# L1f: normalisation and router in one block, six Sinkhorn rounds unrolled on one ScalarE table

## The chip, the core and the metric

The kernel runs on one core of a Trainium2 chip. TensorE multiplies matrices, VectorE and ScalarE work on tiles of 128 partitions, GpSimd does a few small steps and issues the indirect DMAs, and SyncE issues most other DMAs. The metric is the device time of one execution in microseconds (us); the median of several runs counts.

## The reference, cut to what matters

The model is a decoder of four layers, each with self-attention, cross-attention and an expert network, over 8 x 256 tokens of 128 numbers. The change lies in the expert network of layer 1 (L1f), in which experts choose tokens after a Sinkhorn normalisation of the router's scores:

```python
def _sinkhorn(logits, n_iters=6, tau=1.0):
    t = logits / tau
    for _ in range(n_iters):
        t = t - logsumexp(t, axis=-2, keepdims=True)   # over the 16 experts of a token
        t = t - logsumexp(t, axis=-1, keepdims=True)   # over the 256 tokens of an expert
    return jnp.exp(t)

x = x + L1_ffn(layernorm(x))
# in L1_ffn, with x normalised:
gate_logits = einsum('bnd,ed->ben', x, gate_query)
affinity = _sinkhorn(gate_logits / exp(log_temp))
gates, idx = top_k(affinity, 32)                       # 32 tokens for each of 8 x 16 pairs
h = gelu(einsum('becd,edf->becf', x[idx], w1) + b1)
expert_out = einsum('becf,efd->becd', h, w2) + b2
out = zeros.at[idx].add(gates * expert_out)
```

## The kernel before, in words

The twelve stages of the decoder run one after another in blocks; at the end of a block all engines meet, and a short block clears its semaphores. x lies in x_sb as 16 tiles of 128 tokens.

L1f is `ffn_choosing_experts`. It first calls `normalize_all` (line 1389), which is a block of its own. VectorE takes the statistics of all 16 tiles (L1406, L1409), adds epsilon (L1411), waits for one power of -1/2 on GpSimd over all tiles (L1420), and writes the normalised tiles xn (L1414). TensorE turns them (L1426), four to a PSUM bank, and ScalarE copies the banks to xT (L1433). SyncE meanwhile loads the router's weights and the temperature and stores x to DRAM.

The second block holds everything else. TensorE multiplies the 16 tiles of xT with the router (L2591; an f32 matmul shows as two instructions). VectorE divides by the temperature into by_token (L2480), in which 128 tokens lie on the partitions and 16 x 16 values beside each. Then a hardware loop runs the six rounds on four engines. By token: maximum (L2486), subtract (L2488), Exp on ScalarE (L2563), sum (L2490), Ln on ScalarE (L2565), subtract (L2492). TensorE turns the values into PSUM (L2596), so that each of the 128 (sequence, expert) pairs has a partition with its 256 tokens. By pair: maximum (L2495), its negative (L2497), Exp with the sum taken along (L2567), Ln (L2570), one subtraction of both (L2499). TensorE turns back into PSUM (L2601), and VectorE copies that to by_token (L2502). Each step waits for the one ahead of it, on a semaphore and a register that counts rounds (`wait_step`).

After the rounds ScalarE takes Exp (L2572), and VectorE finds the 32 best of each pair in four passes (from L2509). The picks are spread over the partitions (L2610), VectorE turns them into one-hot tiles `hot` (L2529), and TensorE gathers the chosen rows by multiplying xn with them (L2618). Ahead of the gathers stand 12 matmuls of no use but to keep TensorE busy (`keep_clock`, L1386). Then 16 experts follow: hidden (L2630), Gelu on ScalarE (L2584), back to model width (L2642), bias and gate on VectorE (L2542, L2550), and two indirect DMAs on GpSimd that add the result into two sums in DRAM (L2466). SyncE loads expert weights into a ring of four and, when `blank` has been zeroed by GpSimd (L2456), clears the second sum. The two sums come back and are added into x_sb.

L3f, the last stage, is not touched. It normalises in two halves within the block of its router, with 20 `keep_clock` matmuls at its head.

Of the kernel before, what the change touches and what calls it, by code (L numbers as in the profile page):

```python
# [46 lines left out]
def wait_step(eng, step, b, k):  # L47

    eng.wait_ge(step.sem, step.after(b, k))
# [2315 lines left out]
def ffn_choosing_experts(nc, x_sb, const, w, cfg, follow):  # L2365
# [11 lines left out]
    with ExitStack() as ctx:  # L2377
# [8 lines left out]
        normalize_all(nc, x_sb, xn, xT, const, cfg["name"] + "ln_", [("x", sum_dram[0])], stored,  # L2386
                      [(w_r[:], w["w_r"], loaded), (temp[:, 0:1], w["log_temp"].broadcast_to([P, 1]), temp_in)])
# [12 lines left out]
        pair_small = sb("pair_small", [P, 4])  # L2400
# [14 lines left out]
        tok_dve, tok_act = sem.step("tok_dve", 5), sem.step("tok_act", 2)  # L2415
        to_pair, to_token = sem.step("to_pair", 1), sem.step("to_token", 1)
        pair_dve, pair_act = sem.step("pair_dve", 3), sem.step("pair_act", 2)
# [13 lines left out]
        with nc.Block() as block:  # L2431

            @block.sync
            def _(sp):
                sem.start(sp)
                sp.dma_start(b_1[:], w["b_1"].rearrange("e p c -> p e c")).then_inc(biases, 16)
                sp.dma_start(b_2[:], w["b_2"].rearrange("(a e) d -> a (e d)", a=1).broadcast_to([P, E * P])).then_inc(biases, 16)
                for e in range(E):
                    if e >= W_RING:
                        sp.wait_ge(y_full, e - W_RING + 1)  # L2440
                    sp.dma_start(w_1[:, e % W_RING, :], w["w_1"][e]).then_inc(w_in[e % W_RING], 16)
                    sp.dma_start(w_2[:, e % W_RING], w["w_2"][e]).then_inc(w_in[e % W_RING], 16)
# [12 lines left out]
            def _(pool):  # L2455
                pool.memset(blank[:], 0.0).then_inc(blanked, 1)  # L2456
# [13 lines left out]
            def _(dve):  # L2470
# [3 lines left out]

                dve.wait_ge(start, 1)
# [3 lines left out]
                for q in range(QT):  # L2479
                    dve.tensor_scalar(by_token[:, q * B:(q + 1) * B, :],  # L2480
                                      ps[:, 0, 0:NT * E].rearrange("p (b q e) -> p q b e", b=B, q=QT)[:, q], temp[:, 2:3],
                                      None, ALU.mult).then_inc(start, 1)
                dve.wait_ge(start, 2 + QT)
                with dve.Fori(0, ROUNDS) as r:

                    dve.tensor_reduce(tok_small[:, 0], by_token[:], AX, ALU.max).then_inc(tok_dve.sem, 1)  # L2486
                    wait_step(dve, tok_dve, r, 1)
                    dve.tensor_tensor(lowered[:], by_token[:], spread(tok_small[:, 0]), ALU.subtract).then_inc(tok_dve.sem, 1)  # L2488
                    wait_step(dve, tok_act, r, 1)
                    dve.tensor_reduce(tok_small[:, 1], exps[:], AX, ALU.add).then_inc(tok_dve.sem, 1)  # L2490
                    wait_step(dve, tok_act, r, 2)
                    dve.tensor_tensor(by_token[:], lowered[:], spread(tok_small[:, 2]), ALU.subtract).then_inc(tok_dve.sem, 1)  # L2492

                    wait_step(dve, to_pair, r, 1)
                    dve.tensor_reduce(pair_small[:, 0:1], ps[:, 1, 0:S], AX, ALU.max).then_inc(pair_dve.sem, 1)  # L2495
                    wait_step(dve, pair_dve, r, 1)
                    dve.tensor_scalar(pair_small[:, 1:2], pair_small[:, 0:1], -1.0, None, ALU.mult).then_inc(pair_dve.sem, 1)  # L2497
                    wait_step(dve, pair_act, r, 2)
                    dve.tensor_scalar(by_pair[:], ps[:, 1, 0:S], pair_small[:, 0:1], pair_small[:, 3:4], ALU.subtract,  # L2499
                                      ALU.subtract).then_inc(pair_dve.sem, 1)  # L2500
                    wait_step(dve, to_token, r, 1)
                    dve.tensor_copy(by_token[:].rearrange("p t e -> p (t e)"), ps[:, 2, 0:S]).then_inc(tok_dve.sem, 1)  # L2502
                    wait_step(dve, tok_dve, r, 5)
# [54 lines left out]
            def _(act):  # L2558
                act.wait_ge(temp_in, 16)
                act.activation(temp[:, 1:2], temp[:, 0:1], ACT.Exp).then_inc(start, 1)  # L2560
                with act.Fori(0, ROUNDS) as r:
                    wait_step(act, tok_dve, r, 2)
                    act.activation(exps[:], lowered[:], ACT.Exp).then_inc(tok_act.sem, 1)  # L2563
                    wait_step(act, tok_dve, r, 3)
                    act.activation(tok_small[:, 2], tok_small[:, 1], ACT.Ln).then_inc(tok_act.sem, 1)  # L2565
                    wait_step(act, pair_dve, r, 2)
                    act.activation(pair_exps[:], ps[:, 1, 0:S], ACT.Exp, bias=pair_small[:, 1:2],  # L2567
                                   accum_out=pair_small[:, 2:3]).then_inc(pair_act.sem, 1)
                    wait_step(act, pair_act, r, 1)
                    act.activation(pair_small[:, 3:4], pair_small[:, 2:3], ACT.Ln).then_inc(pair_act.sem, 1)  # L2570
                wait_step(act, pair_dve, ROUNDS, 0)
                act.activation(aff[:, 0, :], by_pair[:], ACT.Exp).then_inc(aff_done, 1)  # L2572
# [15 lines left out]
            def _(pe):  # L2588
                pe.wait_ge(loaded, 16)
                for t in range(NT):  # L2590
                    last = pe.matmul(ps[:, 0, t * E:(t + 1) * E], xT[:, t * P:(t + 1) * P], w_r[:], start=True, stop=True)  # L2591
                last.then_inc(logit_full, 1)
                with pe.Fori(0, ROUNDS) as r:
                    wait_step(pe, tok_dve, r, 4)
# [3 lines left out]
                    last.then_inc(to_pair.sem, 1)  # L2598
                    wait_step(pe, pair_dve, r, 3)
                    for q in range(QT):  # L2600
                        last = pe.transpose(ps[:, 2, q * P:(q + 1) * P], by_pair[:, q * P:(q + 1) * P], const["ident"][:])  # L2601
                    last.then_inc(to_token.sem, 1)
# [45 lines left out]
                keep_clock(pe, const, ps[:, 0, :], 12)  # L2648
# [1039 lines left out]
```

## Time and profile before

| | us |
|---|---|
| median of 3 runs | 2680.62 |
| lowest and highest run | 2675.12, 2686.98 |
| span of the profiled execution | 2693.3 |
| of it L1f, from its first instruction to the next stage | 1176.7 to 1361.1 |

TensorE is busy for 84% of the span, VectorE for 58%, ScalarE for 50%. These shares are means over twelve stages with different limits, so the stretch of L1f has to be read by itself: the rows below come from there, and from L3f where it does something of a like form. A row of the timeline has the start, the duration, the engine and line, the operation with what it writes and reads, and in brackets how long the engine was idle ahead of it and what released it. PEclk is the clock granted to TensorE: 1.00 is 2.4 GHz and 0.50 is 1.2 GHz.

### The profile page before, as it was taken

Reading aid. Unit: us, or ns where it says so; the run is one execution under the profiler, and the core shown is the slowest. Engines: PE = TensorE matmul, PEld = TensorE weight load, DVE = VectorE, ACT = ScalarE, POOL = GpSimd, SP = SyncE. Lnnn points to the kernel's source line nnn. Section 1 sums busy time; section 2 is a strip of 40 time slices with the busy share of each in tenths; the row PEclk is TensorE's granted clock in tenths of the full one; section 3 lists DMA queues with packets and bytes.
Section 4 is the critical chain, followed back from the end, with each engine's and each line's share of the span. In section 5 each row is a group of like instructions: output and inputs, shape, how many; then the busy total and the mean of one; then the engine's idle time right before and its main releaser. Section 6 shows DMA issues by size and latency. Waiting matters only on the chain. (4 is left out here: it accounts for less than half of the span.)

```text
span 2693.3 us, 48335 instructions
## 1 busy us (share of the span) xinstructions
PE 2274.5 (84%) x16465; PEld 1476.8 (55%) x16465; DVE 1567.7 (58%) x4625; ACT 1336.8 (50%) x3615; POOL 714.3 (27%) x981
## 2 busy tenths in 40 slices
PE   6969997789898499953859999867968999799999
PEld 4635543755555155531747676556846776366653
DVE  4757772246666687734256674543457775777730
ACT  3726661136554276645436776322335565366642
POOL 2122212444443323100723331233412111322100
PEclk9979998879998699976979999978979999799989
DMA  2023326120000233230610000253410000433200
GB/s 74 2 79 96 100 52 195 41 63 32 33 17 17 55 107 89 76 100 0 125 44 1 1 1 1 95 131 108 139 53 1 2 2 2 111 84 84 63 18 16
DMA packets 126656, 155.77 MB, mean 58 GB/s; under 512 B 22592, under 2 KB 89289, under 8 KB 125266
## 3 DMA queue, kind: packets, MB, share of 16 engines
q1 hardware_dynamic: 113858, 141.30, 18.3%
q0 software_dynamic: 8640, 8.31, 1.5%
q10 hardware_dynamic: 3920, 3.09, 0.6%
q8 instruction: 136, 2.23, 0.3%
q14 instruction: 102, 0.84, 0.1%
HBM read 117.83 MB, written 35.51 MB: 57 GB/s over the span
## 5 line engine op out<-in xcount | busy, mean ns | idle before, releaser
L584 ACT ACTIVATE L3x_p_ring<-L3x_ps_t 128x512 f32<-128x512 f32 x256 | 141.7, 598 | 105.8 <-PE L3x_ps_t L663 104.7
L467 DVE CUSTOM_DVE_ANT_0 L3x_ps_s<-L3x_ps_s,L3x_mask_q 128x512 f32<-128x512 f32 x256 | 170.0, 717 | 35.0 <-PE L3x_ps_s L642 33.6
L584 ACT ACTIVATE L1x_p_ring<-L1x_ps_t 128x512 f32<-128x512 f32 x256 | 137.5, 621 | 76.3 <-PE L1x_ps_t L661 76.3
L584 ACT ACTIVATE L0x_p_ring<-L0x_ps_t 128x512 f32<-128x512 f32 x256 | 137.5, 623 | 73.1 <-PE L0x_ps_t L661 73.1
L470 DVE TENSOR_REDUCE L0x_mx<-L0x_ps_s 128x2 f32<-128x1024 f32 x128 | 151.8, 1221 | 34.3 <-PE L0x_ps_s L642 33.8
L470 DVE TENSOR_REDUCE L1x_mx<-L1x_ps_s 128x2 f32<-128x1024 f32 x128 | 151.9, 1221 | 28.4 <-PE L1x_ps_s L642 27.1
L1006 ACT ACTIVATE L2a_probs<-L2a_ps_s,L2a_top 128x256 f32<-128x256 f32 x256 | 118.0, 473 | 78.4 <-DVE L2a_top L956 78.4
L661 PE MATMUL L3x_ps_t<-L3x_q_stack,L3x_k_stack 128*128 128x256 bf16 x512 | 120.9, 275 | 5.3 <-DMA L3x_q_stack<-L3x_m_rows 5.0
L1006 ACT ACTIVATE L3a_probs<-L3a_ps_s,L3a_top 128x128 f32<-128x128 f32 (+1 forms) x256 | 104.2, 423 | 38.2 <-DVE L3a_top L952 36.1
L663 PE MATMUL L3x_ps_t<-L3x_mask_k,const_ident_bf 128*128 128x256 bf16 x512 | 120.5, 275 | 0.0
L890 POOL COPY L3a_wide<-L3a_inverse 128x128 f32<-128x128 f32 x128 | 33.8, 293 | 226.6 <-DVE L3a_inverse L969 226.6
L661 PE MATMUL L0x_ps_t<-L0x_q_stack,L0x_k_stack 128*128 128x256 bf16 x512 | 85.5, 277 | 8.1 <-DMA L0x_q_stack<-L0x_m_rows 4.3
L642 PE MATMUL L3x_ps_s<-L3x_k_stack,L3x_q_stack 125*128 125x512 bf16 x256 | 80.6, 397 | 13.7 <-DMA L3x_q_stack<-L3x_q_dram 9.6
L642 PE MATMUL L0x_ps_s<-L0x_k_stack,L0x_q_stack 125*128 125x512 bf16 x256 | 80.8, 399 | 13.1 <-DMA L0x_q_stack<-L0x_q_dram 9.0
L642 PE MATMUL L1x_ps_s<-L1x_k_stack,L1x_q_stack 125*128 125x512 bf16 x256 | 80.8, 398 | 12.4 <-DMA L1x_q_stack<-L1x_q_dram 8.5
L952 DVE CUSTOM_DVE_ANT_0 L3a_ps_s<-L3a_ps_s,const_causal_min 128x128 f32<-128x128 f32 (+1 forms) x256 | 83.9, 390 | 12.2 <-PE L3a_ps_s L1085 12.2
L661 PE MATMUL L1x_ps_t<-L1x_q_stack,L1x_k_stack 128*128 128x256 bf16 x512 | 85.2, 277 | 6.6 <-DMA L1x_q_stack<-L1x_m_rows 3.0
L1386 PE MATMUL L1a_ps_p<-const_some_rows,const_ones_bf 128*128 128x512 bf16 x265 | 76.0, 397 | 17.0 <-DVE L1a_w_cs L2907 17.0
L956 DVE TENSOR_REDUCE L2a_top<-L2a_ps_s 128x2 f32<-128x512 f32 x128 | 81.9, 681 | 12.4 <-PE L2a_ps_s L1085 12.4
L1915 DVE TENSOR_TENSOR L2f_hid<-L2f_gated,L2f_ps 128x256 f32<-128x256 f32 (+1 forms) x93 | 38.6, 419 | 79.1 <-ACT L2f_gated L1976 56.8
L974 DVE TENSOR_TENSOR L2a_oT<-L2a_ps_o,L2a_spread 128x256 f32<-128x256 f32 x64 | 27.1, 423 | 95.5 <-ACT L2a_spread L1023 83.2
L1976 ACT ACTIVATE L2f_gated<-L2f_ps 128x256 f32<-128x256 f32 (+1 forms) x93 | 35.0, 383 | 93.5 <-PE L2f_ps L2036 39.9
(717 smaller groups left out, 6112.1 us busy)
## 6 DMA issues: line engine op xcount, KB each, us to landing
L2f_w_e<-L2f_in_w_e SPq DMA_DIRECT2D x23, 544.0 KB
L0x_k_stack<-L0x_k_dram SPq DMA_DIRECT2D x96, 96.0 KB
L1x_k_stack<-L1x_k_dram SPq DMA_DIRECT2D x96, 96.0 KB
L3x_k_stack<-L3x_k_dram SPq DMA_DIRECT2D x96, 96.0 KB
L0f_w<-L0f_in_w SPq DMA_DIRECT2D x32, 256.0 KB, 4.6
L1a_rk_wide<-L1a_rk_dram SPq DMA_DIRECT2D x8, 1024.0 KB
L1f_w<-L1f_in_w SPq DMA_DIRECT2D x32, 256.0 KB
kept_x<-ctxT SPq DMA_DIRECT2D x24, 256.0 KB, 3.5
```

What stands on the lines that cost most here:

```text
L467: last = dve.tensor_tensor_reduce(span, span, mask_q[:, t, :], 1.0, 2 * MASKED, ALU.add, ALU.max, accum_out=mx[:, t, k:k + 1])
L470: last = dve.tensor_reduce(mx[:, :, k], s_bank(o), AX, ALU.max)
L584: act.activation(p_ring[:, u % RING, j * BANK:(j + 1) * BANK], t_bank(o), ACT.Exp, scale=scale).then_inc(out["t"].sem, 1)
L642: last = pe.matmul(s_bank(o)[:, t, :], q_stack[0:MAX_ROW, par, k, t * P:(t + 1) * P], k_stack[0:MAX_ROW, par, k, :], start=True, stop=True)
L661: last = pe.matmul(dst, k_stack[:, par, u, kt * P:(kt + 1) * P], q_stack[:, par, u, :], start=True, stop=not masked)
L663: last = pe.matmul(dst, const["ident_bf"][:], mask_k[:, kt, :], start=False, stop=True)
L952: last = dve.tensor_tensor_reduce(span, span, const["causal_min"][:, S - keys_of(t):S], 1.0, -2 * MASKED, ALU.add, ALU.min, accum_out=top[ ...
L956: dve.tensor_reduce(top[:, slot, j, :], bank.rearrange("p (t k) -> p t k", t=QT), AX, ALU.min).then_inc(top_done, 1)
L1006: last = act.activation(probs[:, n % P_RING, t, 0:keys_of(t)], ps_s[:, n % s_banks, S * t:S * t + keys_of(t)], ACT.Exp, scale=-1.0, bias=t ...
L1386: pe.matmul(bank, const["ones_bf"][:], wide, start=True, stop=True)
L1915: dve.tensor_tensor(hid[0:rows, n % 2, i, :], gated[0:rows, m % H_RING, :], h_bank(m)[0:rows, TILE:2 * TILE], ALU.mult).then_inc(h_out, 1)
L1976: act.activation(gated[0:rows, m % H_RING, :], h_bank(m)[0:rows, 0:TILE], ACT.Silu).then_inc(gate_out, 1)
```

## The change

- The normalisation moves into the router's block and runs in two halves of eight tiles; GpSimd takes a power for each half. Turning, copying and router matmuls of four tiles each interleave on TensorE. 16 `keep_clock` matmuls stand at the head of TensorE's list.
- ScalarE loads one table by name at the start, which is to serve Exp and Ln, and the table of Gelu right after the last Exp of the rounds.
- The rounds are written out six times, with waits on constants.
- All values are negated: maxima become minima, Exp takes a scale of -1, and the minimum is itself the bias of the pair's Exp, so that the negation L2497 goes.
- The values turned back stay in PSUM (`turned_back`) and are read there by the minimum and the subtraction; the copy L2502 goes. The last round turns nothing back.
- The 12 `keep_clock` matmuls move from behind the first spread of picks to right behind the rounds.
- GpSimd zeroes `blank` when the router's scores are there; SyncE issues the loads of weights and biases at the start of the common block.

```diff
-        normalize_all(nc, x_sb, xn, xT, const, cfg["name"] + "ln_", [("x", sum_dram[0])], stored,
-                      [(w_r[:], w["w_r"], loaded), (temp[:, 0:1], w["log_temp"].broadcast_to([P, 1]), temp_in)])
...
+        turned_back = ps[:, 2, 0:S].rearrange("p (t e) -> p t e", e=E)
...
             @block.sync
             def _(sp):
                 sem.start(sp)
+                sp.dma_start(w_r[:], w["w_r"]).then_inc(loaded, 16)
+                sp.dma_start(temp[:, 0:1], w["log_temp"].broadcast_to([P, 1])).then_inc(temp_in, 16)
+                sp.dma_start(sum_dram[0].rearrange("(t p) d -> p t d", p=P), x_sb[:]).then_inc(stored, 16)
...
             @block.gpsimd
             def _(pool):
+                for half in range(2):
+                    tiles = slice(half * NT // 2, (half + 1) * NT // 2)
+                    pool.wait_ge(stat_steps, (half + 1) * (NT + 1))
+                    pool.tensor_tensor(rstd[:, tiles], mean_var[:, tiles, 1], const["minus_half"][:, tiles], ALU.pow).then_inc(powered, 1)
+                pool.wait_ge(logit_full, 1)
                 pool.memset(blank[:], 0.0).then_inc(blanked, 1)
...
+                for half in range(2):
+                    tiles, steps = range(half * NT // 2, (half + 1) * NT // 2), half * (NT + 1)
+                    for n, t in enumerate(tiles):
+                        dve.bn_stats(stats[:, t, :], x_sb[:, t, :]).then_inc(stat_steps, 1)
...
+                for t in range(NT):
+                    dve.wait_ge(powered, t // (NT // 2) + 1)
+                    dve.tensor_scalar(xn[:, t, :], x_sb[:, t, :], mean_var[:, t, 0:1], rstd[:, t:t + 1], ALU.subtract,
+                                      ALU.mult).then_inc(normed, 1)
...
-                    dve.tensor_scalar(by_token[:, q * B:(q + 1) * B, :],
+                    dve.tensor_scalar(turned_back[:, q * B:(q + 1) * B, :],
                                       ps[:, 0, 0:NT * E].rearrange("p (b q e) -> p q b e", b=B, q=QT)[:, q], temp[:, 2:3],
-                                      None, ALU.mult).then_inc(start, 1)
+                                      -1.0, ALU.mult, ALU.mult).then_inc(start, 1)
...
-                with dve.Fori(0, ROUNDS) as r:
...
-                    dve.tensor_scalar(pair_small[:, 1:2], pair_small[:, 0:1], -1.0, None, ALU.mult).then_inc(pair_dve.sem, 1)
...
-                    dve.tensor_copy(by_token[:].rearrange("p t e -> p (t e)"), ps[:, 2, 0:S]).then_inc(tok_dve.sem, 1)
-                    wait_step(dve, tok_dve, r, 5)
+                for r in range(ROUNDS):
+                    if r:
+                        dve.wait_ge(to_token, r)
+                    dve.tensor_reduce(tok_small[:, 0], turned_back, AX, ALU.min).then_inc(tok_low, 1)
+                    dve.wait_ge(tok_low, 2 * r + 1)
+                    dve.tensor_tensor(lowered[:], turned_back, spread(tok_small[:, 0]), ALU.subtract).then_inc(tok_low, 1)
...
             @block.scalar
             def _(act):
+                act.preload_act_table_set("natural_log_exp_and_others")
+                for c in range(4):
+                    act.wait_ge(turned, 4 * (c + 1))
+                    act.activation(xT[:, c * BANK:(c + 1) * BANK], ps[:, 4 + c, :], ACT.Copy).then_inc(copied, 1)
...
+                for r in range(ROUNDS):
+                    act.wait_ge(tok_low, 2 * r + 2)
+                    act.activation(exps[:], lowered[:], ACT.Exp, scale=-1.0).then_inc(tok_exps, 1)
+                    act.wait_ge(tok_sum, r + 1)
+                    act.activation(tok_small[:, 2], tok_small[:, 1], ACT.Ln).then_inc(tok_log, 1)
+                    act.wait_ge(pair_low, r + 1)
+                    act.activation(pair_exps[:], ps[:, 1, 0:S], ACT.Exp, bias=pair_small[:, 0:1], scale=-1.0,
+                                   accum_out=pair_small[:, 1:2]).then_inc(pair_sum, 1)
+                    act.wait_ge(pair_sum, r + 1)
+                    act.activation(pair_small[:, 2:3], pair_small[:, 1:2], ACT.Ln).then_inc(pair_log, 1)
+                act.wait_ge(pair_ready, ROUNDS)
+                act.activation(aff[:, 0, :], by_pair[:], ACT.Exp, scale=-1.0).then_inc(aff_done, 1)
+                act.preload_act_table(ACT.Gelu_apprx_tanh)
...
+                keep_clock(pe, const, ps[:, 1, :], 16)
+                for c in range(4):
+                    for t in range(4 * c, 4 * c + 4):
+                        pe.wait_ge(normed, t + 1)
+                        pe.transpose(ps[:, 4 + c, (t % 4) * P:(t % 4 + 1) * P], xn[:, t, :], const["ident"][:]).then_inc(turned, 1)
+                    if c == 0:
+                        pe.wait_ge(loaded, 16)
+                    else:
+                        logits(c - 1)
+                logits(3)
...
+                    pe.wait_ge(pair_ready, r + 1)
+                    if r + 1 < ROUNDS:
+                        for q in range(QT):
+                            last = pe.transpose(ps[:, 2, q * P:(q + 1) * P], by_pair[:, q * P:(q + 1) * P], const["ident"][:])
+                        last.then_inc(to_token, 1)
+                keep_clock(pe, const, ps[:, 0, :], 12)
                 pe.wait_ge(top, 3 * (CAP // 8) + 2)
...
                 spread_picks(0)
-                keep_clock(pe, const, ps[:, 0, :], 12)
```

## Rows read from the trace of the kernel before

**Rows 1.** Windows of L1f: busy us (count) of PE, PEld, DVE, ACT, POOL; PEclk:

```profile
1190.00:1197.20 7.20, 6.98 (x32) 6.90 (x32) 0.17 (x1) 1.49 (x2) 1.80 (x1) 0.50 0.76 224
1207.10:1216.10 9.00, 1.37 (x4) 0.58 (x4) 3.23 (x8) 6.53 (x9) 0.00 (x0) 0.50 0.16 58
1290.00:1337.00 47.00, 46.41 (x324) 43.66 (x322) 12.81 (x41) 21.28 (x52) 39.37 (x26) 1.00 0.77 159
```

**Rows 2.** Timeline of L1f's scatters and expert start, after the gathers:

```profile
1283.38 2.05 PE L2642 MATMUL L1f_ps<-L1f_w,L1f_hT 128*128 128x128 f32 x16 [0.41 <-ACT L1f_hT L2584]
...
1287.35 1.71 POOL L2466 DMA_INDIRECT L1f_sum_even<-L1f_y,L1f_pick_col  x1 [95.40 <-DVE L1f_y L2550]
```

**Rows 3.** Timeline of L1f, last scatter:

```profile
1345.14 1.55 POOL L2466 DMA_INDIRECT L1f_sum_odd<-L1f_y,L1f_pick_col  x1 [0.30 <-issue]
```

**Rows 4.** Timeline of L1f, start of norm and router's matmuls:

```profile
1176.69 3.19 DVE L1406 BATCH_NORM_STATS2 L1f_ln_stats<-x_sb 128x6 f32<-128x128 f32 x16 [0.75 <-PEq L104]
...
1190.19 6.98 PE L2591 MATMUL L1f_ps<-L1f_w_r,L1f_xT 128*128 128x16 f32 x32 [1.28 <-PEq L104]
```

**Rows 5.** Timeline of L3f, from its first statistics to its last router matmuls:

```profile
2594.18 1.65 DVE L1524 BATCH_NORM_STATS2 L3f_stats<-x_sb 128x6 f32<-128x128 f32 x8 [1.03 <-PEq L104]
2594.19 7.17 PE L1386 MATMUL L3f_ps<-const_some_rows,const_ones_bf 128*128 128x512 bf16 x20 [1.50 <-PEq L104]
...
2604.76 1.99 PE L1611 MATMUL L3f_ps<-L3f_w_r,L3f_xT 128*128 128x32 f32 x16
```

**Rows 6.** Windows of L3f, columns as in rows 1:

```profile
2599.00:2600.00 1.00, 1.00 (x5) 0.34 (x3) 1.00 (x5) 0.00 (x0) 1.00 (x1) 0.67 0.89 352
2606.00:2607.00 1.00, 0.75 (x7) 0.61 (x6) 0.93 (x3) 0.00 (x0) 0.00 (x0) 0.74 0.00 0
2613.00:2614.00 1.00, 1.00 (x5) 0.33 (x5) 0.00 (x0) 0.00 (x0) 0.00 (x0) 0.84 0.00 0
```

**Rows 7.** Timeline of the second round, up to the third's first step:

```profile
1208.48 1.28 ACT L2565 ACT_TABLE_LOAD   x1
1208.49 0.42 DVE L2490 TENSOR_REDUCE L1f_tok_small<-L1f_exps 128x16 f32<-128x256 f32 x1 [0.48 <-ACT L1f_exps L2563]
...
1210.01 1.28 ACT L2567 ACT_TABLE_LOAD   x1
...
1211.68 0.15 DVE L2497 TENSOR_SCALAR L1f_pair_small<-L1f_pair_small 128x1 f32<-128x1 f32 x1
1211.87 0.47 ACT L2567 ACTIVATE L1f_pair_exps<-L1f_ps,L1f_pair_small 128x256 f32<-128x256 f32 x1 [0.58 <-DVE L1f_pair_small L2497]
...
1212.46 1.28 ACT L2570 ACT_TABLE_LOAD   x1
...
1215.31 0.42 DVE L2502 COPY L1f_by_token<-L1f_ps 128x256 f32<-128x256 f32 x1 [0.78 <-PE L1f_ps L2601]
1216.13 0.42 DVE L2486 TENSOR_REDUCE L1f_tok_small<-L1f_by_token 128x16 f32<-128x256 f32 x1 [0.39 <-DVE L1f_by_token L2502]
```

**Rows 8.** Instructions on by_token and pair_small: ns min/median/max, first and last start:

```profile
L2486 DVE TENSOR_REDUCE L1f_tok_small<-L1f_by_token x6: 419/420/421, 1198.1 to 1243.1; 128x16 f32<-128x256 f32 x6
...
L2495 DVE TENSOR_REDUCE L1f_pair_small<-L1f_ps x6: 424/424/426, 1202.2 to 1247.2; 128x1 f32<-128x256 f32 x6
```

**Rows 9.** Timeline behind the last round:

```profile
1249.97 0.54 DVE L2499 TENSOR_SCALAR L1f_by_pair<-L1f_ps,L1f_pair_small 128x256 f32<-128x256 f32 x1 [2.15 <-ACT L1f_pair_small L2570]
...
1251.25 0.42 ACT L2572 ACTIVATE L1f_aff<-L1f_by_pair 128x256 f32<-128x256 f32 x1
...
1251.92 0.43 DVE L2509 MAX8 L1f_gates<-L1f_aff 128x8 f32<-128x256 f32 x1 [0.21 <-DVE L1f_by_token L2502]
```

**Rows 10.** Timeline of the first gather:

```profile
1259.38 3.87 PE L1386 MATMUL L1f_ps<-const_some_rows,const_ones_bf 128*128 128x512 bf16 x12
...
1259.63 1.41 DVE L2529 TENSOR_SCALAR L1f_hot<-L1f_ps,const_row_numbers 128x512 f32<-128x512 f32 x2 [1.13 <-PE L1f_ps L2610]
...
1263.30 1.88 PE L2618 MATMUL L1f_ps<-L1f_hot,L1f_xn 128*128 128x512 f32 x4
```

More of the change, by code:

```diff
@@ L2385, in ffn_choosing_experts @@
         loaded, temp_in, stored = sem("loaded"), sem("temp_in"), sem("stored")
-        normalize_all(nc, x_sb, xn, xT, const, cfg["name"] + "ln_", [("x", sum_dram[0])], stored,
-                      [(w_r[:], w["w_r"], loaded), (temp[:, 0:1], w["log_temp"].broadcast_to([P, 1]), temp_in)])
+        stats = sb("stats", [P, NT, 6])
+        mean_var = sb("mean_var", [P, NT, 2])
+        rstd = sb("rstd", [P, NT])
         w_1 = sb("w_1", [P, W_RING, HID])
@@ L2472, in spread @@
                     return a.rearrange("p (t a) -> p t a", a=1).broadcast_to([P, QT * B, E])
+                for half in range(2):
+                    tiles, steps = range(half * NT // 2, (half + 1) * NT // 2), half * (NT + 1)
+                    for n, t in enumerate(tiles):
+                        dve.bn_stats(stats[:, t, :], x_sb[:, t, :]).then_inc(stat_steps, 1)
+                    for n, t in enumerate(tiles):
+                        dve.wait_ge(stat_steps, steps + n + 1)
+                        dve.bn_aggr(mean_var[:, t, :], stats[:, t, :]).then_inc(stat_steps, 1)
+                    dve.wait_ge(stat_steps, steps + NT)
+                    dve.tensor_scalar(mean_var[:, tiles[0]:tiles[-1] + 1, 1], mean_var[:, tiles[0]:tiles[-1] + 1, 1], EPS, None,
+                                      ALU.add).then_inc(stat_steps, 1)
+                for t in range(NT):
+                    dve.wait_ge(powered, t // (NT // 2) + 1)
+                    dve.tensor_scalar(xn[:, t, :], x_sb[:, t, :], mean_var[:, t, 0:1], rstd[:, t:t + 1], ALU.subtract,
+                                      ALU.mult).then_inc(normed, 1)
                 dve.wait_ge(start, 1)
@@ new lines, in _ @@
+                for r in range(ROUNDS):
[4 more added lines that the diff above has]
+                    dve.tensor_tensor(lowered[:], turned_back, spread(tok_small[:, 0]), ALU.subtract).then_inc(tok_low, 1)
+                    dve.wait_ge(tok_exps, r + 1)
+                    dve.tensor_reduce(tok_small[:, 1], exps[:], AX, ALU.add).then_inc(tok_sum, 1)
+                    dve.wait_ge(tok_log, r + 1)
+                    dve.tensor_tensor(by_token[:], lowered[:], spread(tok_small[:, 2]), ALU.add).then_inc(tok_ready, 1)
+                    dve.wait_ge(to_pair, r + 1)
+                    dve.tensor_reduce(pair_small[:, 0:1], ps[:, 1, 0:S], AX, ALU.min).then_inc(pair_low, 1)
+                    dve.wait_ge(pair_log, r + 1)
+                    dve.tensor_scalar(by_pair[:], ps[:, 1, 0:S], pair_small[:, 0:1], pair_small[:, 2:3], ALU.subtract,
+                                      ALU.add).then_inc(pair_ready, 1)
@@ L2588, in _, with logits @@
             def _(pe):
[L2589 to L2594, printed above, removed]
+                def logits(c):
+                    pe.wait_ge(copied, c + 1)
+                    for t in range(4 * c, 4 * c + 4):
+                        last = pe.matmul(ps[:, 0, t * E:(t + 1) * E], xT[:, t * P:(t + 1) * P], w_r[:], start=True, stop=True)
+                    if c == 3:
+                        last.then_inc(logit_full, 1)
+                keep_clock(pe, const, ps[:, 1, :], 16)
+                for c in range(4):
+                    for t in range(4 * c, 4 * c + 4):
+                        pe.wait_ge(normed, t + 1)
[5 more added lines that the diff above has]
+                logits(3)
+                for r in range(ROUNDS):
+                    pe.wait_ge(tok_ready, r + 1)
                     for q in range(QT):
@@ L2597, in _ @@
                                             by_token[:, q * B:(q + 1) * B, :].rearrange("p b e -> p (b e)"), const["ident"][:])
[L2598 to L2602, printed above, removed]
+                    last.then_inc(to_pair, 1)
+                    pe.wait_ge(pair_ready, r + 1)
[4 more added lines that the diff above has]
+                keep_clock(pe, const, ps[:, 0, :], 12)
                 pe.wait_ge(top, 3 * (CAP // 8) + 2)
```

36 lines of the change are left out of this document (6 added, 30 removed).

## The prediction

> **What bounds the kernel now.** I read the busy shares of the page first, then windows over L1f, then its timeline. The page's 84% for TensorE says little here: L1f lasts from 1176.7 to 1361.1, and its first half is a chain in which one engine works at a time. The windows show it: in a round of 9.00 us TensorE works 1.37, VectorE 3.23 and ScalarE 6.53, of which most is table loads, while TensorE's clock stands at 0.50, its lower level of 1.2 GHz [rows 1]. So in this half every microsecond taken from the chain is taken from the stage.
>
> The second half is bound elsewhere. TensorE looks like the limit of the experts (46.41 of 47.00 us) [rows 1], but the end of the stage is set by GpSimd's 32 scatters: the first starts at 1287.35, released by VectorE's first y [rows 2], the last at 1345.14 after a gap of 0.30 [rows 3]. That is 57.79 us for 31 steps, 1.86 each, the 1.55 of a scatter plus 0.30, with no room for a wait. So the chain starts with the first y and then runs by itself, and whatever brings the first y forward brings the end of L1f, and all stages behind it, forward by as much. I therefore sum how much earlier the first y comes. The terms are read from one execution with a span of 2693.3 us; the median of the runs is 2680.62, 12.7 less, and I take the same difference off both.
>
> **The change part by part.**
>
> *Norm and router.* Now the router's matmuls end at 1190.19 + 6.98 = 1197.17, which is 20.48 us after the first statistics at 1176.69 [rows 4]. L3f already does what the change does: halves, no block border, warm-up matmuls, turning and router matmuls interleaved. It starts at 2594.18 and its last router matmuls end at 2604.76 + 1.99 = 2606.75, so it takes 12.57 [rows 5]. It has 20 warm-ups in 7.17 us, to 2601.36 [rows 5]; L1f will have 16. The clock rose at about 2599.66, as the stretch 2599 to 2600 has a mean of 0.67 [rows 6]: 5.47 us low and 1.70 high, so 0.44 a warm-up at the low clock and 0.22 at the high one, and four fewer save 0.9. The new head takes 11.7, and **8.8 us** go. Bounds: TensorE's work behind the warm-ups took 2606.75 - 2601.36 = 5.39 at the high clock. If the clock stays low throughout, that doubles to 10.8 behind at most 7.2 of warm-ups, 18.0 in all, and 2.5 are gained. If it is high from the first warm-up on, 16 of them take 3.5 instead of 6.3, and 2.8 more are gained at most (VectorE's tiles would be late next).
>
> Queues: SyncE issues the weights some 13 us earlier, behind the router's loads, and then stands at `blanked` as now. GpSimd's zeroing of `blank` (its 1.80 busy us in the first window [rows 1]) waits for the scores; behind it SyncE holds the clearing of the second sum and the weights of the next stage, which nobody needs for some 90 us, and GpSimd holds only the scatters. The zeroing now lies beside VectorE's first round. No row shows the two delaying one another; I take 0, with 1.8 as the bound. The Exp of the temperature stands behind ScalarE's four copies, beside the last router matmuls, and costs nothing; without them it would cost a few tenths.
>
> *A round.* Four table loads lie in each, 1.28 us each. Two are on the path. The Ln of the tokens has its load at 1208.48, done at 1209.76; its sum is ready at 1208.49 + 0.42 = 1208.91 [rows 7], so without the load Ln starts at about 1208.94: **0.82**. The Ln of the pairs waits for nothing but its load at 1212.46 [rows 7]: **1.28**. The two loads of Exp, of which one stands at 1210.01 [rows 7], run while VectorE and TensorE work, and removing them brings nothing; the cover is the 1.86 us from that load's start to its Exp at 1211.87, which turning and maximum fill; with the loads gone it hides nothing else. The negation goes, from 1211.68 to the Exp at 1211.87: **0.19**. The copy and the loop's end go, from 1215.31 to the next maximum at 1216.13: **0.82** [rows 7]. Together 3.11 of a round of 9.00, which leaves 5.9. The first maxima start at 1198.1 and 1243.1, five rounds apart, so all rounds are alike [rows 8]. Five times 3.11, and 2.29 for the last, whose copy and exit are counted below: **17.8 us**.
>
> What is added is small. Minimum and subtraction read PSUM instead of SBUF: a maximum of 128x256 from SBUF took 420 ns and one from PSUM 424 [rows 8], 0.05 us for twelve such steps. The Trainium skill speaks against this part: "VectorE: DVE Perf Modes", section on the TRN2 errata, gives a VectorE step 58 cycles before its data from SBUF and 120 from PSUM at 0.96 GHz. By that page twelve steps would cost an estimated 0.8 us more; the rows named just now don't show it. Writing out the rounds lengthens the engines' programs; the whole rest of L1f is written out and its steps follow each other as closely, so I take 0. If TensorE's high clock outlasted the head, at most half of its 1.37 us a round [rows 1] would go, 4.1 us in six; I take 0, since L3f's clock fell in the stretch 2606 to 2607 (mean 0.74), as its router matmuls ended [rows 6].
>
> On the loads the skill has a second price: "ScalarE: Activation LUTs", section "What ACT_TABLE_LOAD costs", puts a switch at 1283 ns plus a drain of 1380. By it the two switches on the path would give an estimated 16 us more over six rounds. The trace has no such drain: the Exp behind a load follows it by what its input needs, and a whole round is 9.00 us.
>
> *Behind the rounds.* by_pair ends at 1249.97 + 0.54 = 1250.51; then comes a load, the Exp at 1251.25, and the first pass of the best at 1251.92 [rows 9], 1.41 later. Without load, and without the last turn and copy, it is the Exp's 0.42 and two hand-overs of 0.04: 0.5, so **0.9 us** go.
>
> *Warm-ups ahead of the gathers.* They fill TensorE from 1259.38 to 1263.25, and the first gather starts at 1263.30, though its first half of `hot` is done at about 1259.63 + 0.70 = 1260.3 [rows 10]. Moved behind the rounds they lie beside the search for the best, over 7 us long (1251.92 [rows 9] to 1259.63 [rows 10]), while twelve at 0.44 take 5.3: free there, and 2.9 earlier here if the clock is up. If it isn't, the first gather's 1.88 [rows 10] doubles and only 1.0 is left. What TensorE's clock does between the new place and the gather no row shows. I take the middle, **2.0**.
>
> *Gelu's table* is loaded beside the search instead of ahead of the first Gelu. What is late next is TensorE, which is then still at the second expert's hidden layer: it was idle for Gelu only 0.41 us [rows 2]. So **0.4**, between 0 and 0.41.
>
> Sum: 8.8 + 17.8 + 0.9 + 2.0 + 0.4 = **29.9 us**: a span of 2663.4, and a median of 2680.6 - 29.9 = **2650.7**. Lower bound of the gain: 2.5 + 17.8 - 1.8 - 0.1 + 0.9 + 1.0 = 20.3 (2660.3); upper: 11.6 + 17.8 + 4.1 + 0.9 + 2.9 + 0.4 = 37.7 (2642.9).
>
> **The rivals.** *Low clock in the head and at the gather.* The warm-ups don't lift the clock in time, or it falls in the thin router matmuls. For it: L3f's clock fell while those ended [rows 6]. Against it: it stayed up until they did. 29.9 - 6.3 - 1.0 = 22.6 gained, 2658.0. Chance 0.10.
>
> *The loads stay.* The table named at the start doesn't serve both functions, and each switch is still loaded. Then 2.10 a round come back, 12.6 us: 17.3 gained, 2663.3. For it only that each function brings its own table now [rows 7]; 0.04.
>
> *The front was hidden.* Something other than y sets the scatters' start, the clearing of the second sum for one: no gain, 2680.6. Against it stands the releaser of the first scatter [rows 2]; 0.02.
>
> *Slower: the clock stays low through gathers and experts*, as the warm-ups no longer stand right ahead of them. Eight gathers like the first lose 1.88 each, 15.0; the experts' 46.41 us of work double, so that TensorE takes the end from the scatters. The last two scatters (3.7) would then end at 1337.0 + 46.4 + 3.7 = 1387.1 instead of 1346.7, 40.4 later. With 15.0, less the 27.9 gained elsewhere, that is 27.5 slower: 2708. It decides only if the low clock covers gathers and most of the experts. Against it: in L3f, with TensorE busy, the clock had come back in the stretch 2613 to 2614 (0.84) [rows 6]. 0.02.
>
> **How the numbers follow.** My forecast has 0.82. The bounds of its terms reach from 2642.9 to 2660.3, the loads that stay to 2663.3, so the range is 2642 to 2664. Half a per cent, about what a measurement of this kernel can tell from no change, is 13.4 us: forecast, low clock and kept loads all lie beyond it, faster 0.96; the hidden front is same, 0.02; slower 0.02.
>
> **What would show it.** A round of 5.9 us with no ACT_TABLE_LOAD between the first and the last; scores 11.7 us after the first statistics, and a clock of 1.00 while the router's matmuls run; the first best pass 0.5 us behind by_pair; the first gather at its half of `hot`, with its clock; 32 scatters still 1.86 apart. I am wrong if table loads remain, if the scatters show gaps (then the experts or the weights bind), or if the first y comes some 30 us earlier and the kernel does not end earlier by as much.

## The result and the profile after

In the first comparison the changed kernel took 2644.3 us, median of four runs, against 2682.3 for the kernel before: a ratio of 0.9861 [0.9843 to 0.9879], 38.0 us less. A second comparison (below, label e_after) gave 2651.9 against 2682.1, 0.9890 [0.9874 to 0.9907], 30.2 us less. The profiled execution has a span of 2637.8 us. L1f, between its first statistics and those of the next stage, went from 184.5 to 155.7 us.

The timeline of L1f after the change, its head, answers to [rows 4, 5] (start in us, duration, engine, line; in brackets the idle time before and who ended it):

```profile
1170.19 1.64 DVE L2490 BATCH_NORM_STATS2 L1f_stats<-x_sb 128x6 f32<-128x128 f32 x8 [0.75 <-PEq L104]
1170.19 3.62 PE L1386 MATMUL L1f_ps<-const_some_rows,const_ones_bf 128*128 128x512 bf16 x16 [1.21 <-PEq L104]
...
1175.18 2.12 PE L2628 MATMUL L1f_ps<-const_ident,L1f_xn 128*128 128x128 f32 x8 [1.37 <-DVE L1f_xn L2499]
...
1179.70 1.92 PE L2620 MATMUL L1f_ps<-L1f_w_r,L1f_xT 128*128 128x16 f32 x16
```

The scores are done at 1179.70 + 1.92 = 1181.62, 11.43 us after the first statistics, against 20.48 before. The 16 warm-ups took 3.62: the clock was up from the first of them. The idle 1.37 in front of the turning is then VectorE's.

The second round, up to the third's first step, answers to [rows 7]:

```profile
1188.28 0.42 DVE L2514 TENSOR_REDUCE L1f_tok_small<-L1f_ps 128x16 f32<-128x256 f32 x1 [0.78 <-PE L1f_ps L2643]
...
1189.64 0.42 DVE L2518 TENSOR_REDUCE L1f_tok_small<-L1f_exps 128x16 f32<-128x256 f32 x1 [0.48 <-ACT L1f_exps L2590]
1190.09 0.21 ACT L2592 ACTIVATE L1f_tok_small<-L1f_tok_small 128x16 f32<-128x16 f32 x1 [0.48 <-DVE L1f_tok_small L2518]
...
1192.01 0.47 ACT L2594 ACTIVATE L1f_pair_exps<-L1f_ps,L1f_pair_small 128x256 f32<-128x256 f32 x1 [1.70 <-DVE L1f_pair_small L2523]
...
1192.60 0.20 ACT L2597 ACTIVATE L1f_pair_small<-L1f_pair_small 128x1 f32<-128x1 f32 x1
...
1194.17 0.42 DVE L2514 TENSOR_REDUCE L1f_tok_small<-L1f_ps 128x16 f32<-128x256 f32 x1 [0.78 <-PE L1f_ps L2643]
```

No table load stands in it. The Ln of the tokens starts 0.03 us behind its sum, the Ln of the pairs right behind the pairs' Exp, and a round lasts 1194.17 - 1188.28 = 5.89 us instead of 9.00.

Behind the rounds, to the first gather and the first expert (answers to [rows 9, 10]), with the first and the last scatter [rows 2, 3]:

```profile
1216.41 0.54 DVE L2525 TENSOR_SCALAR L1f_by_pair<-L1f_ps,L1f_pair_small 128x256 f32<-128x256 f32 x1 [0.87 <-ACT L1f_pair_small L2597]
...
1217.01 4.21 PE L1386 MATMUL L1f_ps<-const_some_rows,const_ones_bf 128*128 128x512 bf16 x12 [1.93 <-DVE L1f_by_pair L2525]
...
1217.42 1.28 ACT L2600 ACT_TABLE_LOAD   x1
1217.43 0.43 DVE L2532 MAX8 L1f_gates<-L1f_aff 128x8 f32<-128x256 f32 x1 [0.48 <-ACT L1f_aff L2599]
...
1224.06 0.40 PE L2647 MATMUL L1f_ps<-const_ident,L1f_picks_f 128*32 128x128 f32 x1 [2.84 <-DVE L1f_picks_f L2545]
...
1225.94 3.78 PE L2661 MATMUL L1f_ps<-L1f_hot,L1f_xn 128*128 128x512 f32 x4 [0.42 <-DVE L1f_hot L2552]
...
1229.94 2.02 PE L2661 MATMUL L1f_ps<-L1f_hot,L1f_xn 128*128 128x512 f32 x4
...
1244.12 3.69 PE L2673 MATMUL L1f_ps<-L1f_rowsT,L1f_w 128*128 128x256 f32 x16 [0.78 <-ACT L1f_rowsT L2603]
...
1247.65 1.95 PE L2685 MATMUL L1f_ps<-L1f_w,L1f_hT 128*128 128x128 f32 x16
...
1251.52 1.71 POOL L2478 DMA_INDIRECT L1f_sum_even<-L1f_y,L1f_pick_col  x1 [68.03 <-DVE L1f_y L2573]
...
1309.30 1.55 POOL L2478 DMA_INDIRECT L1f_sum_odd<-L1f_y,L1f_pick_col  x1 [0.30 <-issue]
```

The first gather starts as soon as its half of `hot` is there, but takes 3.78 us where it took 1.88. The windows say why (busy us and count of PE, PEld, DVE, ACT, POOL; then the granted clock):

```profile
1220.00:1222.00 2.00, 1.22 (x6) 0.37 (x4) 1.89 (x7) 0.00 (x0) 0.00 (x0) 1.00 0.00 0
1222.00:1224.00 2.00, 0.00 (x0) 0.00 (x0) 1.90 (x7) 0.00 (x0) 0.00 (x0) 0.85 0.00 0
1226.00:1227.00 1.00, 1.00 (x2) 0.48 (x3) 1.00 (x2) 0.00 (x0) 0.00 (x0) 0.50 0.00 0
```

The warm-ups raised the clock while they ran, ended at 1221.22, and in the 2.84 us until the picks it fell to its lower level, 1.2 GHz. The chain of scatters is as it was: 1309.30 - 1251.52 = 57.78 us against 57.79.

The terms, each between the same two instructions of both profiles:

| us | before | after | gained | predicted |
|---|---|---|---|---|
| first statistics to end of the scores | 20.48 | 11.43 | 9.05 | 8.8 |
| scores to the first minimum (maximum) | 0.93 | 0.76 | 0.17 | 0 |
| six rounds, to the end of by_pair | 52.41 | 34.57 | 17.84 | 17.8 |
| by_pair to the first best pass | 1.41 | 0.48 | 0.93 | 0.9 |
| search for the best | 6.63 | 6.63 | 0 | 0 |
| picks turned to first hidden layer | 20.73 | 20.06 | 0.67 | 2.0 |
| first hidden layer to first scatter | 8.07 | 7.40 | 0.67 | 0.4 |
| sum, first statistics to first scatter | 110.66 | 81.33 | 29.33 | 29.9 |

### The profile page after: what moved, and what is told of

Its sections match the earlier page's. It is cut to its first block and busy times, and to the rows that moved or that the text cites. A ratio compares the mean times of both kernels' runs of the same rounds, so it can differ in the third digit from the quotient of the medians.

```text
span 2637.8 us, 48181 instructions
## 1 busy us (share of the span) xinstructions
PE 2256.8 (86%) x16479; PEld 1468.8 (56%) x16479; DVE 1563.1 (59%) x4614; ACT 1306.0 (50%) x3591; POOL 716.2 (27%) x982
## 3 DMA queue, kind: packets, MB, share of 16 engines
q1 hardware_dynamic: 113858, 141.30, 18.9%
## 5 line engine op out<-in xcount | busy, mean ns | idle before, releaser
L952 DVE CUSTOM_DVE_ANT_0 L3a_ps_s<-L3a_ps_s,const_causal_min 128x128 f32<-128x128 f32 (+1 forms) x256 | 83.9, 390 | 12.2 <-PE L3a_ps_s L1085 12.1
L1085 PE MATMUL L2a_ps_s<-L2a_kT,L2a_qT 64*128 64x256 f32 x512 | 73.6, 406 | 4.0 <-ACT L2a_probs L1006 4.0
```

What stands on the lines that cost most here:

```text
L952: last = dve.tensor_tensor_reduce(span, span, const["causal_min"][:, S - keys_of(t):S], 1.0, -2 * MASKED, ALU.add, ALU.min, accum_out=top[ ...
L1085: last = pe.matmul(ps_s[:, n % s_banks, S * t:S * t + keys_of(t)], qT[rows, par, c, t * P:(t + 1) * P], kT[rows, par, cfg["kchunk"](c), 0: ...
```

## The experiments

In the expectations A is the account that I held, B (and C) its rivals. L1f is measured as above, from its first statistics to those of the next stage.

**c_before: where do the other us of the profiles go?** The two profiled spans differ by 55.5 us, of which the trace of L1f shows 28.8. L2f, which the change doesn't touch, went from 205.3 to 189.9. The kernel before, unchanged, once more:

> The kernel before, unchanged, looked at once more. In the first two profiles L1f itself became 28.8 us shorter, as summed, but the unchanged stage L2f went from 205.3 to 189.9 us: in the kernel before, ScalarE waited 17.9 and 9.4 us there, and TensorE 10.8 and 7.8, for nothing that the profile shows. Theory A (it belongs to the program: where its instructions lie decides when an engine's next stretch of code is fetched): L2f takes about 205 us again, with the same long waits of ScalarE. Theory B (an accident of that one execution): L2f takes about 190 us, and the span is nearer to 2678.

Its span was 2674.0, its time 2676.14, L2f 191.6. Where ScalarE waited, in the first and in the second execution of the kernel before (us in total, times, longest):

```profile
ACT L2f_gated L1976 <- PE L2f_ps L2036: 19.9, 6, 6.2
ACT L2f_gated L1976 <- DMA L1x_q_stack<-L1x_q_dram: 17.9, 1, 17.9
ACT L2f_gated L1976 <- issue: 11.2, 2, 9.4
```

```profile
ACT L2f_gated L1976 <- PE L2f_ps L2036: 22.1, 9, 5.5
ACT L2f_gated L1976 <- DVE L2f_hid L1915: 5.8, 12, 0.5
```

So the waits of 17.9 and 9.4 were an accident of that one execution; its span, 2693.3, lies above every timed run shown. The clock's history in the old head is not fixed either: here the scores came 18.37 us after the first statistics instead of 20.48.

**e_own_tables: what are the loads worth?** Only the naming of the table goes, so that each function brings its own again.

```
-                act.preload_act_table_set("natural_log_exp_and_others")
```

> The change without the line that loads the common table of Exp and Ln, so that each function brings its own table again; all else as changed. Theory A (a load costs its 1.28 us, two of four on the path): a round of 5.9 + 0.82 + 1.28 = 8.0 us, and with the load ahead of the last Exp some 13.4 us more than the change, so about 25 us less than before (ratio 0.991). Theory B (a switch also costs a drain of 1.4 us): a round of 10.8 us and 29 us more than the change, 9 us less than before (0.997). Theory C (the loads lie beside other work): a round of 5.9 and no difference from the change (0.986).

The round took 8.00 us, L1f 169.4, and the kernel 2661.16 against 2679.86, 0.9936 [0.9914 to 0.9959]. ScalarE in one round:

```profile
1198.40 0.42 ACT L2589 ACTIVATE L1f_exps<-L1f_lowered 128x256 f32<-128x256 f32 x1 [0.98 <-DVE L1f_lowered L2516]
1198.83 1.28 ACT L2591 ACT_TABLE_LOAD   x1
1200.13 0.21 ACT L2591 ACTIVATE L1f_tok_small<-L1f_tok_small 128x16 f32<-128x16 f32 x1
...
1202.62 1.28 ACT L2596 ACT_TABLE_LOAD   x1
1203.92 0.20 ACT L2596 ACTIVATE L1f_pair_small<-L1f_pair_small 128x1 f32<-128x1 f32 x1
```

Each Ln follows its load by 0.02 us. The loads cost 8.00 - 5.89 = 2.11 a round, the 0.82 + 1.28 of the prediction, and nothing on top: B, a drain beside each load, falls, and so does C. With the loads back the round is still 9.00 - 8.00 = 1.00 us shorter than before; negation, copy and loop's end were put at 0.19 + 0.82, and no run parts these from each other. L1f came out 13.7 longer than in the first profile of the change. In the timed ratios that step is 11 to 12 us if set against e_after, and more against the first comparison, whose 38 us are the outlier here; A's ratio of 0.991, which lies just outside the interval, had been reckoned from those 38.

**e_after: are 38 us real?** The change itself, unchanged, beside more runs of the kernel before.

> The change, unchanged, timed in more rounds. L1f itself became 28 to 29 us shorter in the traces, the first medians differ by 38. Theory A (all of the gain lies in L1f, the rest of the first difference is scatter of stages that nobody touched): 28 to 31 us less than before, ratio about 0.989, L1f about 156 us long. Theory B (some 9 us more are gained outside L1f, in stages whose start moved): 36 to 40 us less again, ratio 0.986.

2651.9 against 2682.1, 30.2 less; by its interval 25 to 34. L1f took 154.8. Its scores came 11.59 us after the first statistics, with a clock that was low in the first warm-ups:

```profile
1176.61 5.78 PE L1386 MATMUL L1f_ps<-const_some_rows,const_ones_bf 128*128 128x512 bf16 x16 [1.21 <-PEq L104]
1182.22 1.49 PE L2628 MATMUL L1f_ps<-const_ident,L1f_xn 128*128 128x128 f32 x8
...
1232.13 3.68 PE L2661 MATMUL L1f_ps<-L1f_hot,L1f_xn 128*128 128x512 f32 x4 [0.63 <-DVE L1f_hot L2552]
```

This is the head as I had predicted it: 5.78 us of warm-ups, and turning right behind them. The first gather was again slow, but the clock fell later, in windows with columns as above:

```profile
1230.00:1231.00 1.00, 0.32 (x3) 0.30 (x4) 0.62 (x2) 0.00 (x0) 0.00 (x0) 1.00 0.00 0
1232.00:1233.00 1.00, 0.87 (x1) 0.45 (x2) 1.00 (x3) 0.00 (x0) 0.00 (x0) 0.61 0.00 0
```

Here TensorE had stood for 1.75 us ahead of the picks, turned and spread them at 1.00, and lost the clock only as the gather began. With the 12 in this place the first gather took 3.39 to 3.78 us in all five profiles.

**e_head_only and e_rounds_only: do the two halves add?** The first is the kernel before with the new head alone (halves, one block, 16 warm-ups), the second the changed kernel with `normalize_all` and the old router matmuls put back. The edits are the two parts of the diff shown above.

> The kernel before with the new head alone: norm in halves in the common block, the 16 warm-up matmuls, turning and router matmuls interleaved. Rounds, tables, the place of the 12 warm-ups and Gelu's table are as before. Theory A (the terms add): scores some 11.5 us after the first statistics instead of 20.5, a round of 9.0 us, L1f about 175 us, 9 us less than before (0.9966). Theory B (the head's gain comes only with the new rounds, or the weights that are loaded earlier hold something up): less than 5 us.

> The change with the old head: the normalisation is a block of its own again, over all 16 tiles, without the 16 warm-ups. Rounds, tables, the place of the 12 warm-ups and Gelu's table are as changed. Theory A (the terms add): scores 20.5 us after the first statistics, a round of 5.9 us, L1f about 164 us, 20 us less than before (0.9925). Theory B (the two parts help each other, for instance by a clock that the head leaves high): the two alone give clearly less than the whole, under 24 us together.

Head alone: 2673.71, 0.9964 [0.9948 to 0.9980], 8.4 us less at the median; rounds, warm-ups and Gelu's table alone: 2661.52, 0.9926 [0.9911 to 0.9941], 20.6 less. The product of the ratios is 0.9890, which is the whole change in the same comparison. Each interval spans some 4 us to either side, so the halves add as far as this can tell; a coupling of a few us would not show. Predicted were 8.8 and 17.8 + 0.9 + 2.0 + 0.4 = 21.1. The rounds took 9.00 us in the first and 5.89 in the second. In the traces the scores came 12.24 us after the first statistics in the first, where 11.5 had been expected, and 20.47 in the second.

**e_cold_head: what do the 16 warm-ups do?**

```
-                keep_clock(pe, const, ps[:, 1, :], 16)
```

> The change without the 16 warm-up matmuls at the head of TensorE's list. Theory A (they hold the clock that the stage ahead left high): the clock is 0.50 when the first tiles are turned, and the 5.4 us of turning and router matmuls take up to twice as long, so the scores come 14 to 16 us after the first statistics instead of 11.2 to 11.9. Theory B (the turning itself brings the clock, the warm-ups only fill time): 12 us or less.

One run: 2657.99 us, L1f 160.3. The clock stood at 0.50 from the first turning to the scores:

```profile
1185.00:1187.00 2.00, 2.00 (x10) 1.77 (x10) 2.00 (x9) 1.19 (x2) 0.42 (x1) 0.50 1.06 242
1191.00:1193.00 2.00, 2.00 (x12) 2.00 (x11) 0.16 (x1) 0.69 (x2) 0.00 (x0) 0.50 1.05 406
```

The scores came 15.4 us after the first statistics. So merging the blocks and interleaving are worth 20.5 - 15.4 = 5.1 us here (3.0 against the 18.37 of c_before). What the warm-ups add depends on the clock: in the eight profiles that have the new head with them, the scores came after 11.43, 11.59, 11.64, 12.16, 12.20, 12.24, 12.27 and 13.49 us (mean 12.1), so they bring 1.9 to 4.0, 3.3 in the mean. The 13.49 are those of e_warm_back, whose head is the change's own. There the clock was up in the warm-ups and fell among the router's matmuls, with TensorE at work:

```profile
1180.00:1181.00 1.00, 1.00 (x12) 1.00 (x11) 1.00 (x5) 0.32 (x2) 0.00 (x0) 1.00 1.01 418
1181.00:1182.00 1.00, 1.00 (x9) 1.00 (x9) 0.27 (x2) 0.52 (x1) 0.00 (x0) 0.70 1.01 387
```

```profile
1182.55 3.43 PE L2620 MATMUL L1f_ps<-L1f_w_r,L1f_xT 128*128 128x16 f32 x16
```

The last 16 matmuls took 3.43 us there, against 1.92 in the first profile of the change.

**e_warm_back and e_warm_long: the warm-ups ahead of the gathers.** The first puts the 12 back behind the first spread, the second leaves them where the change has them and makes them 22, long enough to reach the picks.

```
-                keep_clock(pe, const, ps[:, 0, :], 12)      (behind the rounds)
+                keep_clock(pe, const, ps[:, 0, :], 12)      (behind spread_picks(0))
```

```
-                keep_clock(pe, const, ps[:, 0, :], 12)
+                keep_clock(pe, const, ps[:, 0, :], 22)
```

> The change with the 12 warm-up matmuls back between the first and the second spread of picks, as in the kernel before. In the trace of the change the clock was down again at the first gather, whose four matmuls took 3.78 us. Theory A (the move frees the place but loses the clock): the first gather starts 2.9 us later behind its picks but takes 1.88, and from the turning of the picks to the first expert's hidden layer it is 20.7 us instead of 20.06, so the move was worth 0.7 us. Theory B (the move brings 2 us or more by itself): 22 us or more.

> The change with 22 instead of 12 warm-up matmuls behind the rounds, so that TensorE is at work until the picks are there. Theory A (the clock falls since TensorE stands idle for 2.8 us ahead of the picks): the granted clock is 1.00 at the first gather, whose matmuls take 1.88 us, and from the turning of the picks to the first hidden layer it is about 18 us instead of 20.06. Theory B (the clock falls anyway, or comes too late): the first gather still takes 3.8 us, and the longer warm-up, where it runs at the low clock, delays the turning of the picks by up to 2.4 us.

One run of each: 2649.54 and 2644.95. In the old place the gather waits for the warm-ups and then runs at the high clock:

```profile
1229.35 4.36 PE L1386 MATMUL L1f_ps<-const_some_rows,const_ones_bf 128*128 128x512 bf16 x12 [0.22 <-issue]
...
1233.76 1.88 PE L2660 MATMUL L1f_ps<-L1f_hot,L1f_xn 128*128 128x512 f32 x4
```

With 22 the clock is 1.00 through the gather's first us, and the gather takes 1.98:

```profile
1231.00:1232.00 1.00, 0.41 (x2) 0.00 (x0) 0.77 (x2) 0.00 (x0) 0.00 (x0) 1.00 0.00 0
1232.00:1233.00 1.00, 0.96 (x2) 0.48 (x3) 1.00 (x2) 0.00 (x0) 0.00 (x0) 1.00 0.00 0
```

From the picks to the first hidden layer it is 21.2 us in the old place and 17.5 with the 22, which delay the picks' turning by 0.66 (18.2 net). Over all profiles at hand the old place gave 20.7, 21.3, 21.2 and 21.2 (mean 21.1), the new one with 12 gave 20.1, 19.2, 20.1, 18.9 and 20.6 (mean 19.8). The move alone is worth 1.3 us, and what it missed is another 1.6.

**e_warm_rounds: the clock in the rounds.** Five warm-ups behind each turning, and 22 behind the rounds.

```
                     last.then_inc(to_pair, 1)
+                    keep_clock(pe, const, ps[:, 3, :], 5)
...
                         last.then_inc(to_token, 1)
+                        keep_clock(pe, const, ps[:, 3, :], 5)
-                keep_clock(pe, const, ps[:, 0, :], 12)
+                keep_clock(pe, const, ps[:, 0, :], 22)
```

> The change with 5 warm-up matmuls behind each pair of turns in the rounds (TensorE is idle there for 2.3 and 3.0 us), and 22 instead of 12 behind the rounds. Theory A (the low clock of the rounds costs what the turns take longer): the clock is 1.00 in the rounds, a pair of turns takes 0.41 us instead of 0.69, a round 5.3 instead of 5.9, the first gather 1.9 instead of 3.8, and L1f is about 150 us long, 5 us less than with the change. Theory B (five warm-ups don't bring the clock, or where it is low they get in the way of the turns): rounds of 5.9 us or more, L1f 154 us or more.

2651.42, 0.9874 [0.9858 to 0.9891], L1f 153.1: half of each account. From the second round's first turning on the clock is 1.00, and a round takes 5.39 (the first 5.90, mean 5.50). But at that clock the 22 warm-ups were done in 4.92 us, 2.13 ahead of the picks (not the 2.6 of the next expectation), and the first gather met a falling clock and took 3.56:

```profile
1205.00:1210.00 5.00, 3.03 (x14) 1.32 (x14) 2.55 (x6) 1.18 (x4) 0.00 (x0) 1.00 0.41 150
1237.00:1238.00 1.00, 0.37 (x3) 0.11 (x1) 0.91 (x2) 0.00 (x0) 0.00 (x0) 0.84 0.00 0
1238.00:1239.00 1.00, 1.00 (x2) 0.48 (x3) 1.00 (x2) 0.00 (x0) 0.00 (x0) 0.50 0.00 0
```

**e_warm_tied: warm-ups tied to VectorE's passes.** As before it, but with 12 behind the rounds, and then five after each of three further passes of the search:

```
+                for k in range(2, 5):
+                    pe.wait_ge(top, 3 * k)
+                    keep_clock(pe, const, ps[:, 0, :], 5)
```

> The change with 5 warm-up matmuls behind each pair of turns in the rounds, 12 behind the rounds, and then 5 behind each of the last three passes of the search for the best, so that they follow VectorE's pace whatever the clock is. With 22 in one piece behind warm rounds they were done 2.6 us ahead of the picks, and the clock was down at the first gather. Theory A (the clock falls in that idle stretch and nowhere else): rounds of 5.5 us, clock 1.00 up to the first gather, which takes 1.9 us; 18 us from the turning of the picks to the first hidden layer, L1f 151 to 152 us, 3 to 4 less than with the change, some 33 us less than before (0.9877). Theory B (thin warm-ups don't hold it): the first gather takes 3.8 us again and L1f 153 us or more.

L1f took 150.6 us, the shortest of all. The clock holds from the rounds into the gather:

```profile
1205.00:1225.00 20.00, 11.12 (x52) 4.62 (x50) 9.66 (x23) 5.59 (x20) 0.00 (x0) 1.00 0.00 0
1228.00:1235.00 7.00, 5.68 (x23) 2.02 (x22) 6.09 (x19) 0.00 (x0) 0.00 (x0) 1.00 0.00 0
```

```profile
1201.63 0.44 PE L2637 MATMUL L1f_ps<-const_ident,L1f_by_token 128*128 128x128 f32 x2 [1.51 <-DVE L1f_by_token L2520]
...
1234.05 1.98 PE L2666 MATMUL L1f_ps<-L1f_hot,L1f_xn 128*128 128x512 f32 x4 [0.63 <-DVE L1f_hot L2552]
```

A turning takes 0.44 instead of 0.69, a round 5.39 (the first 5.78, mean 5.46), and the first gather 1.98. From the picks to the first hidden layer it is 17.5 us, with no delay of the picks: 2.3 less than the mean with the 12. The whole kernel took 2645.7 against 2680.27, 0.9865 [0.9843 to 0.9886]. That interval overlaps the 0.9874 to 0.9907 of e_after, so the 4 to 5 us over the change are shown in the trace of L1f, of one execution, and not in the whole time.

## Why the prediction was right, and where it was not

*The bound.* The time goes by the first y. It came 29.3 us earlier in L1f, the 32 scatters behind it took 57.8 us in both (57.8 to 58.0 in all twelve profiles), and the stage got shorter by 28.8; the 0.6 between lie behind the last scatter, which the next stage follows after 16.6 instead of 16.0. The hidden front and the slow end, at which the experts would have taken the end from the scatters, did not occur: the clock was back by the second gather (2.02 us) in the first profile and in e_after.

*The rounds* (17.8 predicted, 17.84 found) were right by their parts: e_own_tables gives back 2.11 a round, the two loads on the path and no more. The drain that the Trainium skill, "ScalarE: Activation LUTs", section "What ACT_TABLE_LOAD costs", adds to a switch does not show here: the loads were 1.28 us, and what followed them stood 0.02 behind. Nor did the Trainium skill's "VectorE: DVE Perf Modes", section on the TRN2 errata, come true for the values in PSUM: the minimum takes 424 to 425 ns there, against 420 from SBUF [rows 8]. Nor does the time go into the gap: from the start of the maximum or minimum to the start of the sum it is 1.36 us with SBUF (1207.13 to 1208.49 [rows 7]) and with PSUM (1188.28 to 1189.64). The maximum of that round before:

```profile
1207.13 0.42 DVE L2486 TENSOR_REDUCE L1f_tok_small<-L1f_by_token 128x16 f32<-128x256 f32 x1 [0.41 <-DVE L1f_by_token L2502]
```

*The head* (8.8 predicted, 9.05 found in the first pair of profiles) was right in size there, by two ways. In e_after the clock rises within the warm-ups, as in L3f, and the scores take 11.59; in the first profile it is up at once, and TensorE then waits 1.37 for VectorE's tile, which the prediction had named as late next: 11.43. I had put 2.8 more as the bound for that history; VectorE leaves next to nothing of it. But neither head is one number. The old one took 20.48, 18.37 and 20.47, the new one 11.4 to 13.5 (mean 12.1), so that over these profiles the term is 7.6 in the mean; that the first pair gave 9.05 is in part luck. In e_warm_back the clock fell among the thin router matmuls, as the rival with 0.10 had it for the head: there the term is still 4.9 to 7.0, not the 2.5 of its lower bound. The zeroing of `blank` beside the first round delayed nothing there: its first reduction takes 0.42, as all others.

*The warm-ups ahead of the gathers* are the term of the sum that was mis-sized: 2.0 predicted, 0.67 in the first profile, 1.3 as a mean of five. I had placed the value in the middle of the bounds, 1.0 and 2.9, for want of a row; the case of the lower bound, a first gather at the low clock, is the one that came, in all five profiles. The rows that I had left aside were L3f's [rows 6], where the clock falls as the work gets thin. Here it fell in the pause of 2.84 us, or, in e_after, after a pause of 1.75 when thin work had begun again. In both the first gather took about twice its 1.88. What the lower bound also lacked in the first profile: the gather starts 2.87 us earlier behind the picks (1.88 instead of 4.75) and loses 1.90, and another 0.30 goes in the second gather and its spread, which still begin at the low clock. e_warm_long and e_warm_tied show that the other end was to be had.

*Gelu's table*: 0.67 instead of 0.4. I had bounded the term by TensorE's idle time of 0.41 in front of one group [rows 2], and that bound was too low: the 16 matmuls of that group start 3.53 instead of 4.10 us behind the start of the hidden layer (0.57), which is 0.16 ahead of its end in the trace instead of 0.41 behind it, and take 1.95 instead of 2.05 (0.10).

*The total.* 2650.7 was predicted, and the two comparisons gave 2644.3 and 2651.9. The terms in L1f come to 29.3, the second comparison to 30.2. The first gave 38.0, a little past the largest gain that I had allowed, 37.7, and the 8 to 9 us more lie in no row of L1f. That the terms sum to 29.3 against 29.9 owes something to chance: the head, Gelu's table and the step ahead of the first minimum made up half of what the warm-ups lacked, and set against c_before, whose head was faster, the sum is 109.15 - 81.33 = 27.8. Stages with the same code in all kernels vary by as much: L1a took between 356.0 and 365.0 us over the twelve profiles. That the 8 us are this scatter fits, but which stage made them in the timed runs can't be read, since only one execution of each has a trace.

## What to carry to other kernels

Where a stage is a chain of short steps on alternating engines, cost each step by the row that it waits for, find what the chain's end sets, and sum only what lies on it: four loads of 1.28 us a round were worth 2.11, not 5.12. Filler that is to hold TensorE's clock must last up to the work that needs it, and a count of matmuls doesn't say how long it lasts, since at the high clock it is over in about half the time (five took 1.24 instead of 2.34 us in e_warm_tied); tie it to the steps of the engine that is waited for. Before a difference of two profiles is explained, look at the stages that the change doesn't touch, and at the same stretch in every profile that has it.

## What the runs showed of the hardware that I had not expected

- Filler of five matmuls behind each thin turning held the granted clock at 1.00 through 20 us of rounds in which TensorE was busy for 11.12, filler included; without it the same rounds ran at 0.50, with 1.38 busy of 5.89.
- After a pause the clock can fall when TensorE is at work again: in e_warm_rounds it stood for 2.13 us, resumed at 1236.44, and the clock fell within 1237 to 1238 (0.84), just ahead of the gather that needed it. In e_after it fell as the gather began, and in the head of e_warm_back among the router's matmuls, after a microsecond with TensorE busy throughout.
- In one execution of the kernel before, ScalarE stood for 17.9 and 9.4 us in L2f, once behind a DMA of an earlier stage by the profile and once behind nothing that it shows; in eleven other profiles L2f took 189.9 to 193.5 us. What it waited for no row shows, and it stays open.
